# First recurrence of a decoder layer: the exponentials of E and n in one ScalarE instruction, the decay's first

## The reference

```python
def step(carry, kv):
    aa, bb, pp = carry
    kt, vt = kv
    qt = jnp.maximum(pp, kt + u)
    e1 = jnp.exp(pp - qt)
    e2 = jnp.exp(kt + u - qt)
    out = (e1 * aa + e2 * vt) / (e1 * bb + e2)
    pp_new = jnp.maximum(pp + neg_ew, kt)
    f1 = jnp.exp(pp - pp_new)
    f2 = jnp.exp(kt - pp_new)
    return ((f1 * aa + f2 * vt, f1 * bb + f2, pp_new), out)
...
k = jnp.einsum('btd,ed->bte', xk, Wk)
v = jnp.einsum('btd,ed->bte', xv, Wv)
r = jax.nn.sigmoid(jnp.einsum('btd,ed->bte', xr, Wr))
wkv = _wkv(time_decay, time_first, k, v)
mu = jnp.mean(wkv, axis=-1, keepdims=True)
var = jnp.mean(jnp.square(wkv - mu), axis=-1, keepdims=True)
ln = (wkv - mu) * jax.lax.rsqrt(var + LN_EPS) * ln_g + ln_b
rwkv = r * ln
return jnp.einsum('btd,ed->bte', rwkv, Wo)
```

## Time and profile before

| | |
|---|---|
| median of 3 executions | 647.29 us (646.05 to 648.07) |
| the profiled execution, its time | 647.78 us |
| its span | 645.7 us, 8051 instructions |
| TensorE busy, matmuls | 549.5 us, 85% of the span |
| VectorE busy | 524.5 us, 81% |
| ScalarE busy | 312.7 us, 48% |
| granted TensorE clock, mean | 0.937 of full |

### The profile page before, as it was taken

The page is one execution under the profiler, slowest core; times in us unless marked ns, Lnnn a source line. Parts: engine busy times, 40 slices in busy tenths (PEclk is TensorE's granted clock), DMA queues, the critical chain, the costliest instruction groups (busy, mean ns, idle before and its releaser), DMA issues.

```text
span 645.7 us, 8051 instructions
## 1 busy us (share of the span) xinstructions
PE 549.5 (85%) x2658; PEld 388.7 (60%) x2658; DVE 524.5 (81%) x935; ACT 312.7 (48%) x508; POOL 23.9 (4%) x39
## 2 busy tenths in 40 slices
PE   3997572279999997789999998789999998799995
PEld 2442331166455776777454767677454767689995
DVE  5999998958998579977999579978999679994433
ACT  4426203237555337736564327745664417753231
POOL 1000000001000000001000000001000000000000
PEclk9999696569999998899999998899999998899999
DMA  8999100010020000020001000011001000000000
GB/s 315 383 358 366 60 1 0 0 34 33 0 62 4 2 32 1 1 67 33 0 17 48 1 16 16 1 65 34 1 3 62 1 3 30 0 33 2 17 17 35
DMA packets 11886, 34.72 MB, mean 54 GB/s; under 512 B 912, under 2 KB 912, under 8 KB 11664
## 3 DMA queue, kind: packets, MB, share of 16 engines
q1 hardware_dynamic: 11856, 34.37, 14.9%
HBM read 30.18 MB, written 12.85 MB: 67 GB/s over the span
## 4 chain that ended last, share of the span: by engine, by line
PE 40%; DVE 35%; issue 15%; ACT 7%; DVEq 1%; DMA 1%; POOL 0%; ACTq 0%; SPq 0%; POOLq 0%
PE gu L467 14%; PE dacc L390 9%; PE bank L376 6%; PE bank L443 6%; PE bank L365 4%; DVE t_slot L668 4%; DVE t_otile L848 2%; DVE t_st L789 2%; DVE t_slot L732 2%; DVE t_stats L641 2%; DVE t_pmax L711 2%; DVE t_slot L740 2%; DVE t_slot L796 2%; DVE t_st L735 2%; DVE t_gap L714 1%
## 5 line engine op out<-in xcount | busy, mean ns | idle before, releaser
L467 PE MATMUL gu<-t_z4h,t_gate 128*128 128x256 f32 x352 | 99.4, 312 | 21.5 <-DVE t_h L830 19.4
L467 PE MATMUL gu<-t_z4l,t_gate 128*128 128x256 f32 x352 | 92.4, 293 | 0.0
L467 PE MATMUL gu<-t_z4h,t_up 128*128 128x256 f32 x352 | 90.3, 288 | 0.0
L467 PE MATMUL gu<-t_z4l,t_up 128*128 128x256 f32 x352 | 90.0, 287 | 0.0
L467 PEld LDWEIGHTS gu<-t_z4h,t_gate 128*128 128x128 f32 x352 | 71.0, 202 | 29.7 <-DVE t_h L830 23.1
L597 ACT ACTIVATE t_silu<-gu,t_fsc 128x256 f32<-128x256 f32 x88 | 41.2, 477 | 91.3 <-PE gu L467 91.0
L390 PE MATMUL dacc<-t_down,t_hh 128*128 128x512 f32 x176 | 73.6, 418 | 5.7 <-DVE t_hl L684 5.7
L489 ACT ACT_TABLE_LOAD x57 | 73.1, 1283 | 1.7 <-PEq L912 0.7
L467 PEld LDWEIGHTS gu<-t_z4l,t_gate 128*128 128x128 f32 x352 | 71.0, 202 | 3.4 <-issue 2.2
L390 PE MATMUL dacc<-t_down,t_hl 128*128 128x512 f32 x176 | 71.7, 407 | 0.0
L830 DVE SCALAR_TENSOR_TENSOR t_h<-gu,t_fsc,t_silu 128x256 f32<-128x256 f32 x88 | 41.8, 477 | 36.4 <-ACT t_silu L597 36.0
(11 more groups left out here) (102 smaller groups left out, 897.3 us busy)
## 6 DMA issues: line engine op xcount, KB each, us to landing
t_xres<-in_x SPq DMA_DIRECT2D x8, 512.0 KB, 3.6
t_mixv<-in_ctx_t SPq DMA_DIRECT2D x4, 1024.0 KB, 5.3
out<-t_otile SPq DMA_DIRECT2D x16, 256.0 KB, 2.1
gate_words<-in_gate_t SPq DMA_DIRECT2D x1, 2816.0 KB, 17.7
up_words<-in_up_t SPq DMA_DIRECT2D x1, 2816.0 KB, 24.0
t_gate<-gate_words SPq DMA_DIRECT2D x1, 2816.0 KB, 16.2
down_words<-in_down_t SPq DMA_DIRECT2D x1, 2816.0 KB, 23.3
t_up<-up_words SPq DMA_DIRECT2D x1, 2816.0 KB, 23.8
```

What stands on the lines that cost most here:

```text
L467: last = pe.matmul(gu[u % 2][:, side, :], as_read(w[:, k, i * P:(i + 1) * P], exact), as_read(part[:, k, hf * HALF:(hf + 1) * HALF], exact ...
```

## The change

In `front`, VectorE writes the decay's argument first, then that of E, then that of n. ScalarE takes the exponential of the decay after the first of them, and after the third one instruction of 1024 elements takes the exponentials of E and n, which lie side by side in `slot`. `exp_done` rises by 2 per chunk instead of 3. In `back`, the first scan waits for both, and the wait ahead of the product is gone. Line numbers behind L553 are up to three lower in the changed kernel (the scan L728 is L726 there, the product L732 is L729, the sum L740 is L737).

```diff
@@ -178,7 +178,7 @@
-        arg_done, exp_done = sem("arg_done", 3 * C), sem("exp_done", 3 * C)
+        arg_done, exp_done = sem("arg_done", 3 * C), sem("exp_done", 2 * C)
@@ -550,11 +550,9 @@
                     table(EXP_SET)
                     sl = slot[:, c % 2]
                     need(act, arg_done, b, 3 * c + 1)
-                    act.activation(sl[:, 0, :], sl[:, 0, :], ACT.Exp, scale=-1.0).then_inc(exp_done, 1)
-                    need(act, arg_done, b, 3 * c + 2)
                     act.activation(fade[:, c % 2, :], fade[:, c % 2, :], ACT.Exp).then_inc(exp_done, 1)
                     need(act, arg_done, b, 3 * c + 3)
-                    act.activation(sl[:, 1, :], sl[:, 1, :], ACT.Exp, scale=-1.0).then_inc(exp_done, 1)
+                    act.activation(sl[:, 0:2, :], sl[:, 0:2, :], ACT.Exp, scale=-1.0).then_inc(exp_done, 1)
@@ -714,8 +712,8 @@
+                    dve.tensor_scalar(fade[:, c % 2, :], gap[:, :], ew[:, c:c + 1], None, ALU.min).then_inc(arg_done, 1)
                     dve.tensor_scalar(sl[:, 0, :], gap[:, :], nw[:, c:c + 1], 0.0, ALU.add, ALU.max).then_inc(arg_done, 1)
-                    dve.tensor_scalar(fade[:, c % 2, :], gap[:, :], ew[:, c:c + 1], None, ALU.min).then_inc(arg_done, 1)
                     dve.tensor_scalar(sl[:, 1, :], gap[:, :], vecs[:, FIRST, c:c + 1], -NEW_CAP,
                                       ALU.subtract, ALU.max).then_inc(arg_done, 1)
@@ -723,11 +721,10 @@
-                    need(dve, exp_done, b, 3 * c + 2)
+                    need(dve, exp_done, b, 2 * c + 2)
                     need(dve, sum_done, b, c)
                     dve.tensor_tensor_scan(st[:, 0, 1:T + 1], decay, sl[:, 0, :], 0.0, ALU.mult, ALU.add).then_inc(scan_done, 1)
                     need_filled(dve, b, "v", c)
-                    need(dve, exp_done, b, 3 * c + 3)
```

## The result

The changed kernel takes 657.11 us in the median of 4 executions (655.56 to 659.27), the kernel before 647.56 beside it (646.05 to 648.07): a ratio of 1.0154, with a 95% interval from 1.0119 to 1.0188. It is slower by 9.5 us. The forecast was 654.2 within 651.0 to 657.6.

What follows compares the result with a forecast made beforehand. VectorE was taken to set the end of the first recurrence, through its sum and ScalarE's tanh to TensorE's transposes. Ten scan delays of 0.69 us, 6.9 in all, on a median of 647.29 gave 654.2 us, range 651.0 to 657.6.

Steps and rivals of the forecast that it cites:

- step 2: ScalarE's merged exponential of E and n starts at T+1.32, released by the third argument; T is the first argument's start.
- step 3: Length D of the 1024-element exponential on ScalarE: 1.04 us, between bounds of 0.61 and 1.23.
- step 4: VectorE's first scan in `back` starts at T+2.39 instead of T+1.70, 0.69 us later, now needing n too.
- step 5: Six places with a `fin` between `front` and `back`: scan starts at T+3.05, 0.66 us of cover remain, no cost.
- steps 1, 6: Decay's argument first, new order of VectorE's arguments and removed wait ahead of the product: worth nothing.
- step 7: ScalarE's next instruction, L515, starts at T+2.26, 0.17 us later; its reader moves back 0.69 itself, so no cost.
- TensorE covers it: Rival: TensorE sets the end of the steady stages, only batch 0 pays, 648.0 us; full coverage 0.05, half 0.08.
- the paragraph behind step 7: TensorE takes over 1.38 us of delay at the gap of `front3` and the third delay at the transposes.
- The sum: Whole kernel: ten scan delays of 0.69 us, 6.9 us, added to the time before, giving 654.2 us.
- Its term for the waits: VectorE's first scan delayed 0.69 us in 10 places, 6.9 us in all.
- a rival with a chance of 0.14: TensorE's clock falls after added idleness, up to 5.2 us more: 655.9 us for one fall, 659.4 for three; chance 0.14.
- ScalarE is the bound: Rival: ScalarE's occupancy by the exponentials counts, so merging saves time: 645.5 us with D at 1.04; chance 0.03.

Runs made afterwards that it cites:

- the order alone: Kernel before with the decay's argument and exponential put first, still three instructions of 512 elements: 647.64 us, ratio 1.0008.
- the runs with the extra work: Overwritten matmuls and repeated transposes keep TensorE busy: changed kernel 655.27 us, the other pair 652.55, kernel before with scan awaiting all three exponentials 651.22, kernel before 647.53.
- the covered ones: VectorE's rest3, prod4, fin0, prod6 moved into the scan's waits: changed kernel 648.11 us, the other pair 646.31, kernel before 645.13.
- the other pair: Kernel before with the exponentials of decay and E merged into one 1024-element instruction, n's following alone: 655.91 us, ratio 1.0140.

## Why the prediction was right, and where it fell short

The time lay in the range, though only 0.5 us under its upper end, and the sign was the one forecast with 0.92. The sum itself was 2.9 us short; the range held the time because it made room for up to two falls of the clock, and that room was needed. Step by step:

- **Start of the merged instruction** (step 2): T+1.32 forecast, T+1.31 measured. The third argument releases it, and ScalarE idles for that.
- **Its length D** (step 3): 1.04 forecast, 1.057 to 1.062 measured in all 16. The slope from 256 to 512 elements held within 0.02.
- **The scan** (step 4): T+2.39 forecast, T+2.40 measured, 0.70 later where 0.69 stood; ten waits together 11.5 us where 11.4 stood.
- **The covered six** (step 5): no wait, as forecast. Three more were covered by moving `fin0`, and the wait went there as well.
- **Nothing for the order** (steps 1, 6): the order alone measured 1.0008. **ScalarE's queue** (step 7): L515 starts at T+2.28, where T+2.26 stood.
- **TensorE covers it**: wrong. The stage grew by 2.12 us per steady batch, all that VectorE lost. The idleness it took is where the paragraph behind step 7 put it: 0.24 and 0.92 us at `r1` and `r2`, where TensorE did not idle before (1.16 for the 1.4 forecast), and 0.71 more before the transposes (0.7 forecast).
- **The sum**: 654.2 forecast, 657.1 measured. Its term for the waits, 6.9, was right at 7.0. What the prediction had named as a sign of being wrong, a clock under 1.00 right behind the first recurrence, was there. The term that was mis-sized is the clock's, put at nothing in the sum: it stood beside it as a rival with a chance of 0.14 and belongs in it. The longer waits leave TensorE idle enough at the transposes that the clock falls in about every second steady batch, 1.5 to 1.6 us each. Three batches, one half, 1.6: 2.4 us, and 7.0+2.4 = 9.4 stands against the measured 9.5. The price of one fall was right (1.7 forecast); what was wrong was to take the fall as a case that happens or does not, because the rows of the kernel before showed none for gaps that short. The Trainium skill's rule (Perfetto Trace Analysis, Matmul Optimizations), that matmuls should run back to back because the engine scales its power with utilization, leaned the right way: the prediction took it to point nearer 659 than 654, and 657.1 is about half way. The half of falls is counted in 12 batches and is a rough figure. That the falls hang on the idleness is shown by the runs with the extra work and the covered ones; that they make up the whole of the remaining 2.5 us is only consistent with the counts and with the speed lost over all executions. For the other pair they do not make up all: with no fall left it still lost 5.2 us for 3.6 of added waits, and those 1.6 us are open.
- **ScalarE is the bound**: wrong. ScalarE waited 27.0 us for the first argument before and after. By the fixed time that the Trainium skill (ScalarE: Activation LUTs, What ACT_TABLE_LOAD costs) puts on each instruction, less the overlap, 1.5 us of ScalarE's time were to be saved. The trace of the change shows no such saving, 313.2 us busy for 312.7, because the long instruction starts only after an idle 0.16 us and overlaps nothing ahead of it; the other pair, with n's exponential right behind, shows just that saving, 311.2. In both the engine waits, and neither run is faster. The Trainium skill's slope and fixed part give 1.04 us for 1024 elements, 0.02 under the measured.

## What to carry to other kernels

Merging two instructions makes every reader wait for the last input of either. Before merging, ask which result is read first and from which input the other part comes; the saving lies on the engine that runs the instruction, the price on the one that reads, and here the first idled and the second set the end of the stage. Work that is already in the reader's queue, moved between the producer's inputs and the reader, was worth more here than the merge: it took back 9.0 of the 9.5 us with the merge in place, and gained 2.3 without it.

## What the runs showed that I had not expected

A small wait can cost twice. An added wait of 3.6 us in ten pieces cost 8.7 us, one of 7.0 cost 9.6, and with TensorE kept busy at the transposes the first cost 5.2: the loss is not in proportion to the wait. A large part of that is the clock: with 1 to 2 us more of idleness per batch it fell in 6 of 12 batches, at a place where it fell in none of 18 without. And these falls differ between executions of the same program: the changed kernel ran in 654.49 us with none behind its first recurrences and in 657.55 with two, its first recurrences being equal to 0.01 us. A single profile of such a kernel tells of one draw.
